# The last batch of a two-layer state-space and expert network in two groups of tokens for three

## What is computed

```python
x = L0_attn_x                                   # (4, 1024, 128)
xn = _layernorm(x)
s = _L0_attn_ref(xn, ...)                       # a scan over time, 256 channels x 16 states
g = _silu(_L0_ffn_ref(xn, ...))                 # 8 experts of width 352, top 2, and a shared one of 192
x = x + s * g
xn = _layernorm(x)
s = _L1_attn_ref(xn, ...)                       # linear attention within each half of the features' heads
g = _silu(_L1_ffn_ref(xn, ...))                 # 8 experts of width 176, top 2, and a gated shared one of 176
x = x + s * g
```

## Time and profile before

| | |
|---|---|
| median of three runs | 1257.25 us (1256.64 to 1262.05) |
| the profiled execution, in all | 1260.23 us |
| its span on the core | 1258.4 us |
| TensorE busy | 930.1 us (74%) |
| VectorE busy | 1022.4 us (81%) |
| ScalarE busy | 612.6 us (49%) |
| GpSimd busy | 599.7 us (48%) |
| mean granted TensorE clock | 0.865 of full |

### The profile page before, as it was taken

The page is one execution under the profiler, slowest core; times in us unless marked ns, Lnnn a source line. Parts: engine busy times, 40 slices in busy tenths (PEclk is TensorE's granted clock), DMA queues, the critical chain, the costliest instruction groups (busy, mean ns, idle before and its releaser), DMA issues.

```text
span 1258.4 us, 16937 instructions
## 1 busy us (share of the span) xinstructions
PE 930.1 (74%) x4540; PEld 656.3 (52%) x4540; DVE 1022.4 (81%) x1808; ACT 612.6 (49%) x1585; POOL 599.7 (48%) x420
## 2 busy tenths in 40 slices
PE   2275677777677668876877879786785898889668
PEld 0053365645455546554654656564553665556446
DVE  4399699989998999877998898889569976877455
ACT  1342554474446545643655565654444554555233
POOL 0137432758425543686336343783865546334500
PEclk9665788897889888998998999999877896888888
DMA  8924334456434333554434434355643346544201
GB/s 265 268 72 99 99 78 100 117 135 155 113 90 104 102 94 102 140 119 138 113 95 113 131 89 117 111 159 133 165 103 99 90 108 153 94 112 112 75 7 30
DMA packets 168650, 144.71 MB, mean 115 GB/s; under 512 B 15680, under 2 KB 135536, under 8 KB 168560
## 3 DMA queue, kind: packets, MB, share of 16 engines
q10 hardware_dynamic: 39168, 67.12, 23.4%
q1 hardware_dynamic: 121712, 60.78, 17.0%
q0 software_dynamic: 7680, 15.74, 4.1%
HBM read 106.88 MB, written 36.70 MB: 114 GB/s over the span
## 4 chain that ended last, share of the span: by engine, by line
DVE 35%; PE 29%; issue 14%; ACT 7%; POOL 6%; SPq 4%; DMA 2%; another core or an unknown queue 1%; ACTq 1%; DVEq 0%; POOLq 0%
DVE pA L1305 11%; PE pM L919 5%; PE pH L829 4%; PE p L884 4%; DVE hj L1341 3%; PE pM L909 3%; POOL dBx L738 3%; POOL gy L712 2%; DVE hc L1313 2%; DVE hj L1353 2%; PE pG L881 2%; SPq L594 2%; PE pH L897 2%; PE pG L884 2%; PE pU L882 2%
## 5 line engine op out<-in xcount | busy, mean ns | idle before, releaser
L738 POOL TENSOR_TENSOR dBx<-dtx,bcb 128x1024 f32<-128x1024 f32 (+1 forms) x144 | 308.4, 2143 | 421.3 <-DMA bcb<-bc_rows 239.7
L829 PE MATMUL pH<-const,hc 128*128 128x128 f32 x1024 | 163.6, 307 | 52.4 <-DVE hc L1313 44.1
L1305 DVE TENSOR_TENSOR_SCAN pA<-pA,carry,dBx 128x512 f32<-128x512 f32 (+1 forms) x160 | 162.9, 1063 | 30.5 <-ACT pA L939 22.2
L939 ACT ACTIVATE pA<-dt,am 128x512 f32<-128x512 f32 (+1 forms) x288 | 173.9, 639 | 22.2 <-DVE hc L1313 13.9
L909 PE MATMUL pM<-const,hj 128*128 128x128 f32 (+3 forms) x636 | 134.3, 310 | 60.0 <-DVE hj L1353 21.6
L1305 DVE TENSOR_TENSOR_SCAN pA<-pA,dBx 128x512 f32<-128x512 f32 x128 | 149.8, 1216 | 33.4 <-ACT pA L939 18.4
L829 PEld LDWEIGHTS pH<-const,hc 128*128 128x128 f32 x1024 | 129.5, 157 | 72.9 <-DVE hc L1313 51.7
L1313 DVE TENSOR_TENSOR hc<-pA,bcb 128x1024 f32<-128x1024 f32 (+1 forms) x144 | 159.3, 1106 | 5.0
L696 POOL DMA_INDIRECT rows_in<-xn,slots x120 | 129.9, 1082 | 58.5 <-DVE expert L1253 29.5
L909 PEld LDWEIGHTS pM<-const,hj 128*128 128x128 f32 (+3 forms) x636 | 76.2, 144 | 136.6 <-issue 91.3
L1111 ACT ACTIVATE yj<-pM 128x128 f32<-128x128 f32 x236 | 65.5, 277 | 159.2 <-PE pM L919 136.3
(11 more groups left out here) (205 smaller groups left out, 1596.4 us busy)
## 6 DMA issues: line engine op xcount, KB each, us to landing
bcb<-bc_rows ACTq DMA_DIRECT2D x112, 512.0 KB
rows_out<-yj SPq DMA_DIRECT2D x236, 64.0 KB
xg<-rows_in SPq DMA_DIRECT2D x176, 64.0 KB
bcb<-bc_rows ACTq DMA_DIRECT2D x32, 256.0 KB
rows_in<-gy SPq DMA_DIRECT2D x8, 512.0 KB, 5.5
mixed<-s_st SPq DMA_DIRECT2D x12, 256.0 KB
so<-rows_out SPq DMA_DIRECT2D x6, 512.0 KB
sr<-mixed SPq DMA_DIRECT2D x6, 512.0 KB
```

What stands on the lines that cost most here:

```text
L738: pool.tensor_tensor(dBx[:, N % 2, :, 0:t1 - t0], dtx[q % 2][:, :, t0:t1], row, ALU.mult).then_inc(dBx_ready, 1)
L829: last = mm(pH[:, half, c * DI + k * P:c * DI + (k + 1) * P], hc[:, N % 2, k, t * P:(t + 1) * P], ident, is_transpose=True, start=(n == 0 ...
L939: A(pA[:, k, 0:t1 - t0], dt[q % 2][:, k, t0:t1], ACT.Exp, scale=am[:, k, n:n + 1]).then_inc(decay_ready, 1)
L1305: dve.tensor_tensor_scan(pA[:, k, 0:w], pA[:, k, 0:w], dBx[:, N % 2, k, 0:w], carry[:, k, N % NS:N % NS + 1] if N in carry_after else 0.0, ...
```

## The change

The last batch is cut into two groups in place of three: tiles 0 to 5 (768 tokens) are routed, with 6 shared and TILES_LAST = 19 routed jobs, and tiles 6 and 7 (256 tokens) are dense over all experts, 18 jobs. The front of the routed group starts at step 129, with six tiles and four scatters a step; that of the dense group stays at step 144. The picker, the step numbers of "mid3" and everything of batches 0 to 2 are as they were. The gathers (12 for 8) and "out3" follow the last routed job by the same rules as before, and there is one "outd" for two. The pieces in which the scan hands over its results keep their three sizes (MIXED_LAST).

```diff
@@ -50,8 +50,10 @@
     return [min(P, width - a) for a in range(0, width, P)]
 
 
-GROUPS = {LAST: (0, CT // 2), LAST + 1: (CT // 2, 3 * CT // 4), LAST + 2: (3 * CT // 4, CT)}
-TILES_LAST = (TOPK * (CT // 2) * P + NE * (P - 1)) // P
+GROUPS = {LAST: (0, 3 * CT // 4), LAST + 1: (3 * CT // 4, CT)}
+MIXED_LAST = [(0, CT // 2), (CT // 2, 3 * CT // 4), (3 * CT // 4, CT)]
+ROUTED_LAST = GROUPS[LAST][1]
+TILES_LAST = (TOPK * ROUTED_LAST * P + NE * (P - 1)) // P
 
 
 def cols(l, b):
@@ -91,7 +93,7 @@
         at(s, "norm", l, b)
         at(s + 1, "xn", l, b)
         at(s + 2, "xT", l, b, 0)
-        if cols(l, b) == (0, CT):
+        if cols(l, b)[1] - cols(l, b)[0] > 4:
             at(s + 3, "xT", l, b, 1)
         else:
             s -= 1
@@ -157,18 +159,17 @@
         at(FFN3_AT + part, "ffn3", part)
     for g, s in enumerate((7 * NS + 1, 8 * NS + 1, STEPS)):
         at(s, "mid3", g)
-    front(1, LAST, 7 * NS + 2, 2)
-    front(1, LAST + 1, 8 * NS + 1, 0)
+    front(1, LAST, 8 * NS + 1, 4)
     for s, *it in ((0, "norm"), (0, "xn"), (0, "xT", 0), (1, "logits"), (1, "top"), (1, "comb")):
-        at(STEPS + s, it[0], 1, LAST + 2, *it[1:])
-    avail[1, LAST + 2, "dense"] = STEPS + 1
+        at(STEPS + s, it[0], 1, LAST + 1, *it[1:])
+    avail[1, LAST + 1, "dense"] = STEPS + 1
     for s, *it in ((2, "gram"), (2, "pm"), (3, "wm"), (3, "attn", 0), (4, "attn", 1)):
         at(STEPS + s, it[0], LAST, *it[1:])
 
     order = [(l, b, kind, i) for l in range(2) for b in range(NB) if (l, b) != (1, LAST)
              for kind, count in (("shared", CT), ("routed", TILES)) for i in range(count)]
-    order += [(1, LAST, kind, i) for kind, count in (("shared", CT // 2), ("routed", TILES_LAST)) for i in range(count)]
-    order += [(1, b, "dense", (t, e)) for b in (LAST + 1, LAST + 2) for t in range(*GROUPS[b]) for e in [NE, *range(NE)]]
+    order += [(1, LAST, kind, i) for kind, count in (("shared", ROUTED_LAST), ("routed", TILES_LAST)) for i in range(count)]
+    order += [(1, b, "dense", (t, e)) for b in (LAST + 1,) for t in range(*GROUPS[b]) for e in [NE, *range(NE)]]
     todo = {0: [j for j in order if j[0] == 0], 1: [j for j in order if j[0] == 1]}
     lanes = {0: [], 1: []}
     starts = {}
@@ -210,11 +211,11 @@
             at(s1 + 6 + part, "combine", 1, b, part)
     s1 = max(last[1, LAST] + 3, STEPS + 1)
     at(s1, "fetch3", 1)
-    for i in range(TOPK * CT // 2):
+    for i in range(TOPK * ROUTED_LAST):
         at(s1 + i // 4, "gather", 1, LAST, i)
     for part in range(6):
         at(max(s1 + 3, STEPS + 5) + part // 2, "out3", part)
-    for b in (LAST + 1, LAST + 2):
+    for b in (LAST + 1,):
         at(max(last[1, b] + 2, STEPS + 5), "outd", b)
 
     plan = [("xload", 0), ("norm", 0, 0), ("xn", 0, 0), ("xT", 0, 0, 0), ("xs", 0, 0), ("xT", 0, 0, 1), ("xs", 0, 1),
@@ -383,7 +384,7 @@
         x0T = [sb("xnT0", [P, L]), sb("xnT1", [P, L])]
         xnT = {(0, b): x0T[b % 2] for b in range(NB)}
         x1T = sb("x1T", [P, L])
-        xnT.update({(1, b): x1T if b < LAST else x0T[0] for b in range(NB + 2)})
+        xnT.update({(1, b): x1T if b < LAST else x0T[0] for b in range(NB + 1)})
         stats = sb("stats", [P, CT, 6])
         mv = sb("mv", [P, CT, 2])
         vpe = sb("vpe", [P, CT])
@@ -706,7 +707,7 @@
                                     pool.wait_ge(out_rows[lane][r], 16 * ((ends[lane, (l, b)] - r + YR - 1) // YR))
                         if b == LAST:
                             if l:
-                                pool.wait_ge(mid3_ready, 1)
+                                pool.wait_ge(mid3_ready, 2)
                         elif n:
                             pool.wait_ge(combined, n)
                     pool.indirect_dma_start(gy3[:, k, c, :] if b == LAST else gy[:, k, c, :], None, rows_out[l][b],
@@ -761,7 +762,7 @@
                     pe.wait_ge(xn_ready, front_no[l, b])
                     take(*("xT", *a))
                     c0, c1 = cols(l, b)
-                    for c in range(min(4, c1 - c0)):
+                    for c in range(min(4, c1 - c0 - 4 * m)):
                         last = pe.transpose(pM[:, c * P:(c + 1) * P], xn[:, c0 + 4 * m + c, :], ident)
                     last.then_inc(bank_full, 1)
                 elif kind == "logits":
@@ -959,7 +960,7 @@
                     l, b, m = a
                     act.wait_ge(bank_full, use["xT", l, b, m])
                     c0, c1 = cols(l, b)
-                    w = min(4, c1 - c0) * P
+                    w = min(4, c1 - c0 - 4 * m) * P
                     A(xnT[l, b][:, c0 * P + m * 512:c0 * P + m * 512 + w], pM[:, 0:w], ACT.Copy).then_inc(bank_read, 1)
                 elif kind == "logits":
                     l, b = a
@@ -1007,7 +1008,7 @@
                             act.wait_ge(mixed_stored, 16 * mix_no[it])
                         A(s_st[:].rearrange("p c d -> p (c d)"), pM[:], ACT.Copy).then_inc(bank_read, 1)
                     elif kind == "mix_out":
-                        c0, c1 = list(GROUPS.values())[a[0] - 2 * LAST]
+                        c0, c1 = MIXED_LAST[a[0] - 2 * LAST]
                         if c0 == 0:
                             act.wait_ge(gathered3, 16 * TOPK * CT)
                         A(s3[:, c0:c1], pM[:, 0:(c1 - c0) * P].rearrange("p (c d) -> p c d", d=P), ACT.Copy).then_inc(bank_read, 1)
@@ -1354,7 +1355,7 @@
                 elif kind == "mid3":
 
                     g, = a
-                    cs = slice(*list(GROUPS.values())[g])
+                    cs = slice(*MIXED_LAST[g])
                     dve.wait_ge(bank_read, use["mix_out", 2 * LAST + g])
                     link(dve.tensor_tensor(gy3[:, 0, cs], gy3[:, 0, cs], s3[:, cs], ALU.mult))
                     dve.scalar_tensor_tensor(out=x[:, cs], in0=gy3[:, 0, cs], scalar=0.5, in1=x[:, cs], op0=ALU.mult, op1=ALU.add
```

## The result

The changed kernel takes 1270.8 us (median of four runs, 1269.3 to 1287.2) against 1257.0 for the kernel before (median of four): ratio 1.013, with an interval from 1.008 to 1.019, slower. Measured again later, it took 1269.3 against 1248.9: 1.016 (1.013 to 1.019). The forecast was 1273, from 1259 to 1286.

The account below looks back on a forecast made before the run. No engine is full, so stages rather than totals were taken to bound the kernel. Three stretches, -11, +7 and +20, gave +16 us, carried over to the median of 1257.25: 1273 us, range 1259 to 1286.

Parts of the forecast that it names:

- A: Scans 112 to 129: the old front's routing and scatters go, 11 us less; ends 5 and 16.
- B: Scans 129 to 143: emptied steps, then a burst on GpSimd, 77 us for 70.0, 7 more; ends 2 and 12.
- The burst: From the slots to scan 143: 21 indirect DMAs at 1.25 us and 4 products at 1.45 on GpSimd, 32.1 us.
- 129 to the slots: From scan 129 until the six tiles' slots are known, summed step by step: 44.9 us.
- C: Scan 143 to the end: more jobs and a wait for gathers, 110 us for 90.0, 20 more.
- Job terms: After scan 143: 15 routed jobs for 8 dense add 13.8 us; early output work moved later takes off 4.7.
- gather term: At step 157 VectorE waits 5.0 us for gathered rows, dense gates queue behind, TensorE drops to half clock: 11 us more.
- Not slower: Rival: first stretch gains its upper end of 16 and no wait arises at step 157; 1260 us, chance 0.13.
- Slower still: Rival: gathers land at their long end and the tail starts at half speed for several jobs; 1285 us, chance 0.15.
- Cheap descriptors: Rival: GpSimd's indirect DMAs not paid one by one, so burst and wait shrink; 1249 us, chance 0.04.
- Less work: Rival: twelve jobs fewer on TensorE save 19 us if its total set the time; 1238 us, chance 0.04.

Follow-up runs that it names:

- e9: The changed kernel itself, unedited, measured and traced again: 1269.3 us, ratio 1.016 to the kernel before.
- e12: The kernel before, unedited, measured again for a second trace: 1250.9 us, ratio 1.001.
- e2: Kernel before, with the third batch's gathers at step 132 instead of 139, and its combination moved with them: 1257.4 us, ratio 1.000.
- e10: Kernel before, with the 16 gathers of its third batch started at step 144, behind the last scan, instead of 139: 1241.1 us, ratio 0.995.
- e6: Kernel before, with only the routed group's front moved from step 114 to 129, its three groups kept: 1291.1 us in one run.
- e5: Changed kernel without the 12 last gathers, so the 768 tokens' output takes stale rows: 1254.7 us, ratio 1.004 to the kernel before.
- e7: Changed kernel with the last 7 dense jobs left out: 1259.6 us in one run.
- e4: Changed kernel with 6 of the last batch's 12 scatters left out (the second choices): 1274.1 us in one run.
- e1: Changed kernel, with the third batch's gathers at step 132 instead of 139, fetches and combination moved too: 1277.0 us, ratio 1.015 to the kernel before.
- e8: Changed kernel, with the third batch's 16 gathers and output work started at step 144 instead of 139: 1258.9 us, ratio 1.006 to the kernel before.
- e11: Changed kernel, with the third batch's gathers at step 144 and the 768 tokens' output parts at steps 160 to 162: 1250.4 us, ratio 1.002.
- e3: Changed kernel, with the 768 tokens' output parts at steps 160 to 162 instead of 157 to 159: 1280.2 us, ratio 1.020.

## Why the prediction was right, and where not

**The sum.** +16 was forecast. The first pair of traces shows +15.7 from scan 112 on; with e9 and e12 the means are 279.4 against 266.0, +13.4; the times +14 and +20. So it is right in its total. Each of the three terms has the sign that was forecast and the mechanism too, with errors that partly cancel.

**A, -11.** The first pair has -15.1, which was to be the upper end. With repeats: four traces of the old code up to step 129 (before, e2, e10, e12) have 98.0 to 106.4, mean 102.0; the nine of the changed kernel's code there have 87.7 to 96.4, mean 91.4. That is -10.6. By these means steps 119 to 122 fell by 6.2 us (7.0 reckoned), steps 117 and 118, with the logits and the top of the old front, by 2.6 (2 reckoned for these and what stands just before them), step 123 by 0.6 (2 reckoned), and the rest by 1.2 in all. The 20.1 us of the first trace against 20.2 worked out from GpSimd's row agree partly by luck: no scan's wait there is put down to GpSimd, and the other eight traces have 18.4 to 20.7. That the cause is the front's place is shown by e6.

**B, +7.** 76.7 and 75.8 for 70.0 and 70.8: +6.7 and +5.0. (From scan 129 to scan 143 there are fourteen steps, 5.0 us each, not fifteen of 4.7; the sum of B is not touched by it.) The burst was reckoned at 32.1 and took 31.9, 31.8, 31.8 (in e5 and e7 as well); 129 to the slots 44.8 for 44.9. e4 and e6 vary its length and give 1.27 and 1.3 us an indirect DMA.

**C, +20.** +24.1 in the first pair, +11.0 in the second (107.8 against 96.8, on two chips), mean 17.6. The 33 jobs I counted for the tail leave out scan 143's own; from there on it is 34 for 27, so the difference of seven was right. Job terms: e5 has 99.4 where they give 99.1. The gather term was 11. Its first sum has a slip: 1.5 + 0.3 + 2 is 3.8 and not 4.1. VectorE asked 16.6 us after the gate of step 153 in e9 (16.1 reckoned), but the rows landed after 24.0 for 21.1: I took TensorE's row to be in SBUF 1.5 us after the gate, and it was 4.5, since TensorE's transposes follow VectorE's gates a slot later, and then the last landing took 2.56 us from the issue's start. So it waited 7.4 for 5.0. TensorE's two jobs at half clock cost 2.4 for 2.8. Against e5 the whole is 8.4: 2.6 less than 11, for the term counted in full what e5 also spends on the parts. In the first trace ScalarE's gaps and a slower start were added, and the near hit of +15.7 there is partly luck: a base that repeats within 7 us was taken from one trace (C 90.0 or 96.8).

**The rivals.** "Not slower" needed A at its upper end and no wait at step 157; the wait was there in all traces with the gathers and with the parts in place. "Slower still" named the mechanism of the first trace's start (half clock for several jobs), at 3.4 us instead of 8. "Cheap descriptors" fell with e4. "Less work" fell with the page of the profile: with 18 us less on TensorE the kernel was slower.

The fit in the Trainium skill, "DMA: Bandwidth & Descriptors", section "Anatomy of one DMA" (2.0 us and 436 GB/s), gives an estimate of 2.15 us for one of these gathers. By the last gather's row in e9 it is 2.56 from the issue's start (1245.44) to VectorE's first use (1248.00).

## What to carry to other kernels

Fewer jobs in all (43 for 55) and less work on three of the four engines made this kernel slower, since seven more of them stood behind the last link of the chain and more indirect DMAs just before it: count what is left there, not the total. When an engine both issues indirect DMAs and feeds the chain, count the operations in its queue from the moment at which the indices are known to the chain's last link; that list times the time of one was the length of the stretch to within 0.3 us where the list was full, and 3 to 5 us short of it where fewer stood there: VectorE's work came last in e1 and e8, and in e6 a fifth product and a wait of 0.87 us for its broadcast row fell into the list. And a wait for gathered rows costs nothing by itself: it costs what is queued behind it on the engine that waits, so put it behind that work (e11), and put gathers that nobody awaits yet behind the chain (e8, e10).

## What was not expected of the hardware

Two traces of the same kernel differ by up to 8 us in one stretch and by under 1 us in the sum (A 106.4 and 98.0, C 90.0 and 96.8), with TensorE's granted clock at 0.75 or 0.56 in the same window of the tail; a gain in one stretch of under about 8 us wants more than one trace. While the twelve last gathers ran, ScalarE was held up for 6.8 to 9.8 us in the sum of its gaps in four traces (the changed kernel's first, e1, e3, e4) and not in four others with the same gathers (e7, e8, e9, e11, all on another chip than e1 to e4), with nothing found in the profile to explain it. Loads of instructions do not sort them: one of these DMAs starts while the gathers run in the first trace, e1 and e3, but also in e8 and e11, and none does in e4. And an indirect DMA that holds GpSimd 0.96 us held it 1.12, 1.87, 1.67 and 1.44 us in e1 where it was issued while a VectorE operation of 1024 elements a row ran (1143.72 to 1144.94 beside the scatter at 1143.95); each of the four ended 0.8 to 0.9 us after that operation. That the one waits for the other is what these rows suggest; it was not tested.
